# GpSimd adds the two key tiles of exponentials per head in images two to four, the denominators multiply the sums behind the values, and a residual moves behind pooling

## The reference

```python
x = x + attention(group_norm(x))      # windowed heads (hifi) and pooled heads (lofi)
x = x + conv3x3(relu(gn * mask(gn)))  # gn = group_norm(x), mask from its centre of mass
...
# the pooled heads, which the change touches
pooled = xh.reshape(B, hg, WS, wg, WS, C).mean(axis=(2, 4)).reshape(B, G, C)
kv = (pooled @ l_kv_w).reshape(B, G, 2, L_HEADS, HEAD_DIM)
attn = jax.nn.softmax(jnp.einsum('bnhd,bmhd->bhnm', q, k) * SCALE, axis=-1)
lo = jnp.einsum('bhnm,bmhd->bnhd', attn, v).reshape(B, H * W, L_DIM)
```

## Time and profile before

| | us |
|---|---|
| median of 3 runs | 343.78 (343.34 to 344.1) |
| the profiled execution | 342.3, its span 340.5 |
| TensorE busy | 308.1 (91%) |
| Vector busy | 270.1 (79%) |
| Scalar busy | 148.8 (44%) |
| GpSimd busy | 87.4 (26%), 47 instructions |
| chain that ended last | PE 51%, DVE 22%, POOL 11%, ACT 8% of the span |

### The profile page before, as it was taken

The page is one execution under the profiler, slowest core; times in us unless marked ns, Lnnn a source line. Parts: engine busy times, 40 slices in busy tenths (PEclk is TensorE's granted clock), DMA queues, the critical chain, the costliest instruction groups (busy, mean ns, idle before and its releaser), DMA issues.

```text
span 340.5 us, 4168 instructions
## 1 busy us (share of the span) xinstructions
PE 308.1 (91%) x1566; PEld 219.1 (64%) x1566; DVE 270.1 (79%) x489; ACT 148.8 (44%) x189; POOL 87.4 (26%) x47
## 2 busy tenths in 40 slices
PE   0998688999799899999799999997999999999995
PEld 1586252488666644887477727886688637878883
DVE  3989699689998687889987769789697667896562
ACT  2553488455726365450258734550354424121300
POOL 6089445214190200009600200029301100202000
PEclk9999999999999999999999999999899999999999
DMA  8746120051000000340103000430001001001003
GB/s 279 284 150 207 39 88 6 0 186 48 0 4 2 0 5 2 124 168 2 65 0 125 1 4 2 157 138 2 4 0 64 0 0 64 0 0 64 0 0 123
DMA packets 12547, 20.48 MB, mean 60 GB/s; under 512 B 2544, under 2 KB 8560, under 8 KB 12272
## 3 DMA queue, kind: packets, MB, share of 16 engines
q1 hardware_dynamic: 12528, 20.23, 16.5%
HBM read 7.93 MB, written 4.19 MB: 36 GB/s over the span
## 4 chain that ended last, share of the span: by engine, by line
PE 51%; DVE 22%; POOL 11%; ACT 8%; issue 6%; DMA 1%; DVEq 0%; POOLq 0%
PE slot L1144 25%; PE cps L1176 14%; PE slot L1220 7%; POOL probs L393 6%; DVE l_max L876 3%; ACT probs L588 3%; PE cps L1220 2%; DVE mask L812 2%; DVE v_lo L842 2%; POOL mask L393 2%; POOL cw_lo L350 1%; PE cps L1144 1%; DMA xy<-x 1%; ACT xn_hi L468 1%; ACT p_w L636 1%
## 5 line engine op out<-in xcount | busy, mean ns | idle before, releaser
L1176 PE MATMUL cps<-v_hi,cw_hi 128*128 128x512 f32 (+1 forms) x144 | 57.6, 400 | 3.7 <-DVE v_lo L842 2.9
L1176 PE MATMUL cps<-v_hi,cw_lo 128*128 128x512 f32 (+1 forms) x144 | 57.8, 401 | 0.0
L1176 PE MATMUL cps<-v_lo,cw_hi 128*128 128x512 f32 (+1 forms) x144 | 56.4, 392 | 0.0
L393 POOL TENSOR_TENSOR probs<-q_w,k_w 128x1024 f32<-128x1024 f32 x14 | 33.0, 2386 | 79.5 <-DVE rw L805 72.3
L588 ACT ACTIVATE probs<-slot 128x1024 f32<-128x1024 f32 x32 | 31.5, 1022 | 14.0 <-PE slot L1144 13.8
L876 DVE TENSOR_REDUCE l_max<-slot 128x4 f32<-128x1024 f32 x32 | 36.8, 1214 | 0.0
L1176 PEld LDWEIGHTS cps<-v_hi,cw_hi 128*128 128x128 f32 x144 | 27.4, 190 | 12.9 <-issue 5.3
L1176 PEld LDWEIGHTS cps<-v_hi,cw_lo 128*128 128x128 f32 x144 | 27.5, 191 | 7.3 <-issue 2.2
L1176 PEld LDWEIGHTS cps<-v_lo,cw_hi 128*128 128x128 f32 x144 | 27.4, 190 | 4.9
L376 POOL TENSOR_TENSOR mask<-rw 128x1024 f32<-128x1024 f32 x8 | 15.2, 1909 | 56.6 <-DVE rw L805 56.6
L1144 PE MATMUL slot<-xn_hi,w_hi 128*128 128x512 f32 (+1 forms) x68 | 27.3, 401 | 0.8 <-DVE xn_lo L734 0.8
(11 more groups left out here) (198 smaller groups left out, 632.7 us busy)
## 6 DMA issues: line engine op xcount, KB each, us to landing
xy<-x SPq DMA_DIRECT2D x8, 512.0 KB, 3.7
out<-xy SPq DMA_DIRECT2D x8, 512.0 KB, 2.6
qs<-probs SPq DMA_DIRECT2D x12, 256.0 KB, 2.5
qs<-probs SPq DMA_DIRECT2D x24, 128.0 KB, 2.1
raw_cw<-conv_w SPq DMA_DIRECT2D x2, 1152.0 KB, 6.2
ks<-probs SPq DMA_DIRECT2D x12, 128.0 KB, 2.1
probs<-h_qkv SPq DMA_DIRECT2D x2, 192.0 KB, 3.9
probs<-l_kv SPq DMA_DIRECT2D x2, 128.0 KB, 3.7
```

Source lines behind the costliest of these rows:

```text
L393: nc.gpsimd.tensor_tensor(product(b, j).rearrange("p (n w) -> p n w", n=NW), q_w[:].rearrange("p (n w) -> p n w", n=NW), k_w[:, j * G:(j + ...
L1176: ins = nc.tensor.matmul(cps[:, pos % 2, y0 * WT:y1 * WT], (cw_hi, cw_hi, cw_lo)[part][:, k, pos, dy + 1, o * P:(o + 1) * P], (v_hi, v_lo, ...
```

## The change

On GpSimd a new function adds the two key tiles of a head: `key_sum[h] = probs[2h] + probs[2h + 1]`. The four sums go to buffers that are free by then: both halves of `mask`, `v_w` and `q_w`. Two of them stand ahead of the pair sum of the windowed values and two behind it. This is done in images 2 to 4; image 1 keeps its 16 denominator matmuls.

On TensorE the denominators of images 2 to 4 are eight matmuls on these sums, and they come behind the values. In images 2 and 3 the window projection follows them; in image 4 it still comes first. The tables put three more convolution matmuls ahead of the pooled projection in images 3 and 4, in image 4 four more besides; in image 2 four more, taken from the places between the last scores.

On Vector, in images 2 and 3, residual 0 moves from ahead of the multiplication to behind the splits, pooling comes next, and residual 1 behind pooling. Scalar waits for the sums before it overwrites the exponentials with the next image.

```diff
@@ -72,7 +72,7 @@
 
 
 EARLY = 8
-REST = (4, 3, 5, 3, 4, 8)
+REST = (4, 3, 5, 3, 4, 11)
 
 
 FRONT = (0, 11, 0, 0, 4, 3, 3, 3, 3, 3, 6, 10, 18)
@@ -80,7 +80,7 @@
 
 
 FRONT_1 = (0, 0, 0, 0, 0, 0, 0, 9, 5, 9, 7, 6, 0)
-REST_1 = (1, 1, 2, 2, 2, 7)
+REST_1 = (1, 1, 2, 2, 1, 11)
 
 
 WARM = (4, 1)
@@ -170,6 +170,7 @@
         v_lo = sb("v_lo", [P, KT, POS, H * WT], F32R)
         mask = sb("mask", [P, KT, HW])
         pv = (q_w[:], k_w[:], xn[:, 0], xn[:, 1])
+        key_sum = (mask[:, 0], mask[:, 1], v_w[:], q_w[:])
         pool_t, pool_s = mask[:, :, 0:2 * G], mask[:, :, 2 * G:3 * G]
 
         raw_cw = nc.alloc_sbuf_tensor_at("raw_cw", [P, KT, ROWS, 3, C], F32, offset=v_at)
@@ -224,6 +225,7 @@
         pv_pool, pv_dve = sem("pv_pool"), sem("pv_dve")
         st_pe, st_exp = sem("st_pe"), sem("st_exp")
         lden_pe, blocks_c, fold_c = sem("lden_pe"), sem("blocks_c"), sem("fold_c")
+        key_sums = sem("key_sums")
         lpv_pe, lnorm = sem("lpv_pe"), sem("lnorm")
         out_pe, y_ready = sem("out_pe"), sem("y_ready")
         yn_ready = sem("yn_ready")
@@ -422,6 +424,11 @@
                     link(weight_low(nc.gpsimd, k, V_SUM, 2), 0)
                     link(weight_low(nc.gpsimd, k, V_DIFF, 0), 0)
 
+            def sum_of_keys(b, h):
+
+                pool.wait_ge(st_exp, b * LT + (h + 1) * MT)
+                nc.gpsimd.tensor_tensor(key_sum[h], probs[:, h * MT], probs[:, h * MT + 1], ALU.add).then_inc(key_sums, 1)
+
             def step(b, first, last):
                 if not first:
                     pool.wait_ge(proj_pe, b * 5 + 5)
@@ -437,8 +444,16 @@
                 else:
                     if b > 1:
                         mask_sum(b - 1, b + 1)
+                    pool.wait_ge(soft_c, (b + 1) * N_SOFT)
+                    pool.wait_ge(v_dve, b * POS)
+                    for h in range(2):
+                        sum_of_keys(b, h)
                     pool.wait_ge(pv_ready, b * NW + 2)
                     nc.gpsimd.tensor_tensor(pv[0], pv[0], pv[1], ALU.add).then_inc(pv_pool, 1)
+                    pool.wait_ge(pv_ready, (b + 1) * NW)
+                    sum_of_keys(b, 2)
+                    pool.wait_ge(pv_dve, (b + 1) * 2)
+                    sum_of_keys(b, 3)
             nc.gpsimd.memset(l_max[:], 0.0).then_inc(zeroed, 1)
             pool.wait_ge(zeroed, 1)
             nc.gpsimd.memset(qs[:].bitcast(F32), 0.0)
@@ -503,6 +518,7 @@
                 for k in range(KT):
                     scaled(b, k, xn).then_inc(xn_ready, 1)
                 act.wait_ge(lpv_pe, b)
+                wait_count(act, key_sums, (b - 1) * HEADS)
                 for k in range(KT):
                     act.wait_ge(xn_ready, b * KT + k + 1)
                     nc.scalar.copy(xn_hi[:, k], xn[:, k]).then_inc(xhi_ready, 1)
@@ -1044,7 +1060,7 @@
                 link(ins)
                 link(nc.vector.reciprocal(inv, blocks[:, :, 0]))
                 link(nc.vector.transpose(blocks, inv.unsqueeze(2).to_broadcast([P, HW // HD, HD])))
-                if not last:
+                if first:
                     residual(b, 0, 1)
                 dve.wait_ge(blocks_c, (b + 1) * N_BLOCKS)
                 dve.wait_ge(lpv_pe, b + 1)
@@ -1056,9 +1072,10 @@
                     last_front()
                     return
                 split_input(b + 1)
+                if not first:
+                    residual(b, 0, 1)
+                    pooling(b + 1)
                 residual(b, 1, 2)
-                if not first:
-                    pooling(b + 1)
                 if not first:
                     conv_result(b - 1, (V_RIGHT,) if b == 1 else (V_LEFT, V_RIGHT))
                 if first:
@@ -1267,15 +1284,27 @@
                               True, True)
                 last.then_inc(st_pe, 1)
 
-            def by_head(s, lhsT, ready):
+            def pooled_values():
 
                 for half in range(2):
                     for t in range(MT):
                         for h in range(HEADS):
-                            last = mm(slot[s][HD * h:HD * (h + 1), half], lhsT(t, h), probs[:, h * MT + t, halves(half)],
+                            head = slice(HD * h, HD * (h + 1))
+                            last = mm(slot[0][head, half], lv[:, t, head], probs[:, h * MT + t, halves(half)],
                                       t == 0, t == MT - 1)
-                    if ready is lden_pe or half == 1:
-                        last.then_inc(ready, 1)
+                last.then_inc(lpv_pe, 1)
+
+            def denominators(b):
+
+                tiles = 1 if b else MT
+                wait_count(pe, key_sums, b * HEADS)
+                for half in range(2):
+                    for t in range(tiles):
+                        for h in range(HEADS):
+                            of = key_sum[h] if b else probs[:, h * MT + t]
+                            last = mm(slot[2][HD * h:HD * (h + 1), half], cst[:, C_ONE:C_ONE + HD],
+                                      of[:, halves(half)], t == 0, t == tiles - 1)
+                    last.then_inc(lden_pe, 1)
 
             def window_scores_of(b, j, to):
 
@@ -1522,14 +1551,19 @@
                     window_out()
                 elif not first:
                     group_means(b + 1, 0)
-                by_head(2, lambda t, h: cst[:, C_ONE:C_ONE + HD], lden_pe)
-                if not last:
+                if first:
+                    denominators(b)
                     window_out()
-                by_head(0, lambda t, h: lv[:, t, HD * h:HD * (h + 1)], lpv_pe)
+                    pooled_values()
+                else:
+                    pooled_values()
+                    denominators(b)
+                    if not last:
+                        window_out()
                 if last:
                     pe.wait_ge(y_ready, B * KT - 1)
                     group_means_of(0)
-                conv.more(fill[5])
+                conv.more(fill[5] + (4 if last else 0))
                 if first:
                     keep_warm(WARM[1])
```

## The result

The changed kernel takes **338.67 us** (median of 6 runs, 337.94 to 340.06); the kernel before, run beside it, 343.1 us (median of 6, 342.31 to 344.1). The ratio is 0.9875, with an interval of 0.9844 to 0.9906: 4.4 us faster, against the 2.8 us forecast. The profiled execution took 338.85 us, its span is 337.0 us at a granted clock of 0.990.

What follows compares the result with a forecast made beforehand. After each image's last exponential, TensorE's gapless chain was taken to bound until the key split hands over to Vector; image 4's end hangs on Vector. Gains 0.1 + 1.8 + 0.9 = 2.8 us off 343.78 gave 341.0 us, range 339.4 to 343.3.

Steps and rivals of the forecast that it cites:

- Part 1, TensorE: Images 2 to 4: eight denominator matmuls instead of 16 save 1.79 us each, up to 5.4 us in all.
- Part 2, the sums: GpSimd's four additions per image take 2.41 us each and hold two-input Vector steps; one chain step passes between sums.
- Image 3: Denominators don't wait, the multiplication L1051 starts at about 203.4 instead of 204.68; gain 1.8 us.
- Part 3, the residual: Vector, images 2 and 3: the moved residual's 1.24 us is covered by idle time ahead of the splits.
- Image 4: Vector's 0.92 us wait for a convolution result goes, the rest becomes TensorE's wait for Vector; gain 0.9 us.
- image 2's normalisation: Vector, image 2: held to 126.4, ends at 128.5, L1051 starts at 131.55; only 0.1 us gained.
- The end with no hold: Image 2 if GpSimd holds nothing: normalisation ends at 124.8, L1051 starts at 130.3; gain 1.2 us.
- The starting point: Whole kernel: the 2.8 us was taken from the shown median of 343.78 us, 1.5 above the profiled execution.
- The bounds: Forecast case from 340.3 to 341.9 us, by image 2's bounds (loss 0.4, gain 1.2) and half of image 4's term.
- GpSimd holds nothing that matters: Rival: image 2's normalisation ends as before, 3.9 us gained in all, 339.9 us; chance 0.18.
- Used up on Vector: Rival: image 3's held normalisation ends another 1.3 us late; only 0.5 us gained in all, 343.3 us; chance 0.20.
- Late sums: Rival: GpSimd sums take 2.99 us each and delay TensorE's denominators; 1.8 us slower, 345.6 us; chance 0.10.

Runs made afterwards that it cites:

- experiment 4: Changed kernel with residual 0 back ahead of the multiplication and pooling back behind residual 1: 340.45 us, 0.9933 of the kernel before.
- experiment 8: Changed kernel with the GpSimd sums of heads 2 and 3 replaced by memsets that read nothing: 339.12 us, 0.9893 of the kernel before.
- experiment 7: Changed kernel with one more GpSimd addition of the same size ahead of each image's last sum: 342.91 us, 1.0003 of the kernel before.
- 5: Changed kernel with the convolution tables of the kernel before: 339.84 us, 0.9907 of the kernel before.
- Kernel 11: Changed kernel with image 4's denominators between its values' halves, 11 convolution matmuls ahead of the projection, and image 2's old table: 337.65 us, 0.9853 of the kernel before.
- 1: The change in image 2 alone, images 3 and 4 as in the kernel before: 342.33 us, 0.9972 of the kernel before.

## Why the prediction was right and wrong

**Direction and mechanism held; the size was 1.6 us short and the time lay under the range's low end.** By the prediction's own steps:

- *Part 1, TensorE.* Eight denominators took 1.83 us, 1.79 had been taken off. The step left out that the new order puts the groups of one shape side by side in images 2 and 3: 2.07 us in image 3, against 1.71 in image 4, where they were neighbours before.
- *Part 2, the sums.* 2.36 to 2.41 us alone, as in the earlier trace rows; 3.43, 2.98 and 2.92 where a Vector sum had the turn first. The denominators' wait was 0.3 us in image 2 (0.4 forecast: 127.01 - 123.26 = 3.75 us behind the start of the values, 3.46 without a wait) and none later. That a chain gets one step between two sums was an assumption, and the trace shows it (1.08, then 2.29 us).
- *Image 3.* L1067 at 203.87 is 203.26 in before's time (this image is 0.61 us late in the profile); forecast 203.4. The term was 1.8 and C is 2.06 shorter; the difference is about the 0.28 us more that TensorE saved.
- *Part 3, the residual.* It fits into the idle time of 1.25 + 0.43 us and of 1.32 us, as reckoned, and experiment 4 prices the move at 0.98 us in image 2 and 0.62 in image 3.
- *Image 4.* Forecast 0.9; E is 0.94 shorter with image 4 alone and 1.11 in the change, with a spread of 0.2. The lost wait at L935 and TensorE's new wait for it are in the rows, and L1067 starts 9.76 us behind the window projection instead of 9.12, 0.6 later as forecast.
- **The step that failed is image 2's normalisation.** It was "held to 126.4", with all eleven steps still to come, and to end at 128.5. In before's time the last sum ended at 126.10, and by then two of the steps were done, one in each gap that a sum left; the chain ended at 127.9. L1067 started at 130.82 and not 131.55. So the "nothing is left of the 1.79 us but 0.1" was 0.81. The end with no hold was right: L1076 of experiment 8 started at 130.23 in before's time, 130.3 had been said. The hold costs image 2 0.4 us, not 1.1. The sum also has no term for the granted clock. B is 0.6 us longer in nine of the ten profiles with image 2 changed, which takes most of that image's gain back, and D is 0.6 us shorter in ten of the eleven with image 4 changed. In the changed kernel the two cancel, and that is luck.
- *The starting point.* The sum was taken from 343.78, the median of three runs; over six, these three among them, it was 343.1, and 342.9 to 343.0 over the 11 to 23 runs beside each later group of kernels. That is 0.7 us of the 2.3 between forecast and measurement; the prediction had noted that the profiled execution was 1.5 under its median. The stages' terms, 3.98 instead of 2.8, are another 1.2 (0.7 of it image 2's, 0.3 image 3's, 0.2 image 4's), and the last 0.4 is within what the granted clock moves from run to run.
- *The bounds.* The forecast's low end of 340.3 does not follow from the terms that it names: image 2's gain of 1.2 us in place of 0.1 leads to 339.9, and half of image 4's term more to 339.4.

Of the rivals, *GpSimd holds nothing that matters* named a time nearer to the result (339.9), yet its mechanism is refuted where it says "nothing holds": the rows and experiment 8 show the hold. What was missed is that most of it falls on time that TensorE spends on the values and denominators anyway. *Used up on Vector* needed the normalisation of image 3 another 1.3 us late and the residual to take all of the idle time. The chain ended at 199.9 in before's time, ahead of the 200.3 forecast, and 0.22 us of idle time is left ahead of the key split. *Late sums* did not occur, and experiment 7 shows its price.

**What stays open** is when the granted clock falls. TensorE pauses ahead of stage B's fall as it does where nothing falls. Its timeline in the change, then in the kernel with images 3 and 4 alone, at the same place:

```profile
163.37 0.48 PE L1350 MATMUL slot<-cst,l_max 128*128 128x128 f32 x1 [1.52 <-DVE l_max L892]
...
164.07 0.61 PE L1193 MATMUL cps<-v_hi,cw_hi 128*128 128x496 f32 x1
```

```profile
163.18 0.33 PE L1361 MATMUL slot<-cst,l_max 128*128 128x128 f32 x1 [1.53 <-DVE l_max L900]
...
163.58 0.39 PE L1203 MATMUL cps<-v_hi,cw_hi 128*128 128x496 f32 x1
```

A matmul takes 0.61 us in the one and 0.39 in the other, after pauses of 1.52 and 1.53 us. Of the ten profiles with image 2 changed nine have the long B (43.43 to 43.54), and one (5) the short; of the three without, none has the long. Kernel 11 has the long B with image 2's old table, so the new table is not its cause. In D the long value stands in the profiles of before, 1 and 5. Whether it is the time at which the pause comes was not tried.

## What to carry to other kernels

Work that is moved to an engine which shares a hold with the chain is priced by what the chain still has to wait for: hold the chain where it would wait anyway, as behind the values here, and most of the hold is free (of 2.4 us in image 2's normalisation the end felt 0.4). When a chain of short steps runs beside long ones of another engine, count the steps that pass in the gaps. And put the operands that come last behind the matmuls that are ready: in three images the same matmuls cost 11 us more where TensorE waited for them, partly since its clock fell in the wait.

## What the runs showed of the hardware

- A GpSimd addition (128x1024, two SBUF operands) and a Vector instruction with two SBUF operands exclude each other in both directions, whoever starts first: a 128x2 step took up to 2.30 us instead of 0.16, a GpSimd sum up to 3.43 instead of 2.36. A GpSimd memset held none of the two-input steps (0.16 us), and one tensor_scalar of 128x2 (int32) for 0.87 to 1.04 us; a GpSimd addition held the same tensor_scalar for 2.22 us in kernel 7.
- After waits of 3.62 and 2.43 us TensorE's granted clock was at 0.50, after 2.06 us it fell in the middle of the work that followed, and after 0.67 and 0.73 us not at all. The short falls of stages B and D cost 0.6 us each, at places where the work is the same in a profile without them.
